# Attention and butterfly feed-forward layer on one core: the output projection moved from step 11 to behind the products with V of step 9, the early projection from step 10 to step 11

## What is computed

```
q, k, v = x·w_q, x·w_k, x·w_v            # 16 heads of 64
p   = softmax(q·k^T / 8 + causal mask)
att = einsum(p·v, w_o)                   # back to 128 features
x   = layernorm(x + att)
h   = butterfly_up(x·W_exp + b_exp)      # 512 features, 9 stages of 2x2 mixes
y   = butterfly_down(gelu(h + up_bias))·W_con + b_con + down_bias
out = layernorm(x + y)
```

## Time and profile before

| | |
|---|---|
| median of 3 runs | 1035.61 us |
| profiled execution, its own time | 1034.01 us |
| its span on the core | 1032.3 us |
| TensorE matmuls busy | 98% of the span |
| TensorE weight loads busy | 68% |
| VectorE, GpSimd, ScalarE busy | 75%, 73%, 59% |
| mean granted TensorE clock | 0.998 |

### The profile page before, as it was taken

How to read it: one execution, slowest core, us unless ns; L and a number is a source line. 1 busy time by engine, 2 the same in 40 slices (tenths; PEclk the granted TensorE clock), 3 DMA queues, 4 the chain that set the end, 5 groups by cost and what they waited for, 6 DMA issues and landing times.

```text
span 1032.3 us, 17783 instructions
## 1 busy us (share of the span) xinstructions
PE 1007.2 (98%) x5832; PEld 698.5 (68%) x5832; DVE 777.4 (75%) x2117; ACT 613.7 (59%) x1246; POOL 750.5 (73%) x715
## 2 busy tenths in 40 slices
PE   7899999999999999999999999999999999999997
PEld 5566676676766676676666766667666766765697
DVE  7867777777777777877788787877778788775456
ACT  4555665566655656666556656666656556665544
POOL 5767888777778887777778887777778887777510
PEclk9999999999999999999999999999999999999999
DMA  5332222233222222232222222332222222320002
GB/s 154 99 99 67 53 69 57 52 83 84 63 63 62 65 70 55 63 83 64 74 72 62 61 54 54 83 83 63 64 62 71 65 56 60 84 63 22 22 11 72
DMA packets 48602, 68.71 MB, mean 67 GB/s; under 512 B 15191, under 2 KB 25083, under 8 KB 48510
## 3 DMA queue, kind: packets, MB, share of 16 engines
q1 hardware_dynamic: 48510, 67.57, 25.4%
HBM read 31.11 MB, written 2.36 MB: 32 GB/s over the span
## 4 chain that ended last, share of the span: by engine, by line
PE 92%; DVE 3%; DMA 2%; ACT 1%; issue 1%; SPq 0%; POOL 0%; POOLq 0%; ACTq 0%
PE O L754 25%; PE WORK L666 14%; PE SC L727 13%; PE SC L733 13%; PE WORK L679 6%; PE WORK L714 3%; PE WORK L639 3%; PE WORK L638 3%; PE WORK L637 3%; PE WORK L815 2%; PE WORK L647 1%; PE WORK L648 1%; PE WORK L649 1%; DVE WORK L1034 1%; DMA R<-RROW 1%
## 5 line engine op out<-in xcount | busy, mean ns | idle before, releaser
L906 ACT ACTIVATE PR<-SC 128x512 f32<-128x512 f32 (+3 forms) x768 | 352.6, 490 | 267.9 <-PE SC L733 242.0
L549 POOL TENSOR_TENSOR SUM<-SUM,PR 128x1024 f32<-128x1024 f32 (+3 forms) x256 | 419.3, 1638 | 14.9 <-ACT PR L906 1.0
L1034 DVE CUSTOM_DVE_ANT_0 WORK<-WORK,CMASK 128x128 f32<-128x128 f32 (+3 forms) x512 | 239.5, 514 | 64.7 <-PE WORK L666 64.6
L727 PE MATMUL SC<-QH,KHL 128*128 128x512 f32 (+3 forms) x768 | 269.2, 356 | 4.2 <-ACT PR L906 4.0
L733 PE MATMUL SC<-QL,KH 128*128 128x512 f32 (+3 forms) x768 | 261.6, 346 | 2.8 <-DMA QL<-NROW 2.8
L534 POOL TENSOR_SCALAR_AFFINE_SELECT PR<-PR 128x256 f32<-128x256 f32 x256 | 105.7, 414 | 192.3 <-ACT PR L906 192.2
L666 PE MATMUL WORK<-KHL,QH 128*128 128x512 f32 (+3 forms) x768 | 224.8, 359 | 2.3 <-DMA KH<-KHL 1.6
L754 PE MATMUL O<-PR,VLO 128*64 128x512 f32 (+3 forms) x1024 | 199.9, 522 | 1.8 <-DVE OT L1121 1.8
L727 PEld LDWEIGHTS SC<-QH,KHL 128*128 128x128 f32 x768 | 145.2, 189 | 62.7 <-ACT PR L906 30.5
L666 PEld LDWEIGHTS WORK<-KHL,QH 128*128 128x128 f32 x768 | 135.4, 189 | 54.0 <-issue 32.6
L1037 DVE TENSOR_REDUCE MP<-WORK 128x1 f32<-128x512 f32 x256 | 164.3, 684 | 4.9
(11 more groups left out here) (134 smaller groups left out, 1103.7 us busy)
## 6 DMA issues: line engine op xcount, KB each, us to landing
QH<-QH SPq DMA_DIRECT2D x128, 128.0 KB, 2.3
KH<-KHL SPq DMA_DIRECT2D x128, 128.0 KB, 2.3
R<-RROW SPq DMA_DIRECT2D x64, 256.0 KB, 3.9
SW<-in_L_ffn_up_weights_dram SPq DMA_DIRECT2D x9, 512.0 KB, 4.4
SW<-_L_ffn_down_weights_dram SPq DMA_DIRECT2D x9, 512.0 KB, 4.4
out_dram<-X SPq DMA_DIRECT2D x7, 256.0 KB, 2.3
X<-in_L_attn_x_BSE_dram SPq DMA_DIRECT2D x3, 512.0 KB, 4.4
X<-in_L_attn_x_BSE_dram SPq DMA_DIRECT2D x2, 256.0 KB, 2.9
```

What stands on the lines that cost most here:

```text
L549: nc.gpsimd.tensor_tensor(total, total, prob(unit, s), ALU.add).then_inc(add_done, 1)
L727: nc.tensor.matmul(dst, KHL[:, par, h, kt * P:(kt + 1) * P], QH[:, par, h, q0:q0 + n], start=True, stop=False)
L906: nc.scalar.activation(prob(unit, s)[:, h, :], SC[use % NSC][:, 0:n], ACT.Exp, scale=K ** -0.5).then_inc(exp_done, 1)
L1034: op = nc.vector.tensor_tensor_reduce(cols, cols, CMASK[:, CH - n:], 1.0, LOWEST, ALU.add, ALU.max, cell)
```

## The change

Two entries of the hand-written order move. In units 0 to 29 the early projection stands behind the scores of step 11, and no longer behind those of step 10. The output projection stands late in step 9, that is directly behind the products with V of steps 4 to 6, and no longer behind the scores of step 11. No instruction is added or taken away. All engines walk through the same table, so ACT's two copies of the early projection and DVE's readout of both move with them, and both take another of the four WORK banks.

```
-FILL[10] = [[], [("proj", 0, 0)], []]
+FILL[11] = [[], [("proj", 0, 0)], []]
 COMPOSE_AFTER = [4, 5, 9]
 RECIP_AFTER = 2
 SCALE_AFTER = 6
-OUT_AT = ((11, 1), (11, 2))
+OUT_AT = ((9, 2), (9, 2))
```

## The result

The median is 1071.68 us (1071.09 to 1072.06, 4 runs) against 1035.61 us before (1035.30 to 1036.40, 4 runs): a ratio of 1.0353, 95% interval 1.034 to 1.0365. The forecast was 1070.3 us. The profiled execution took 1071.44 us, its span 1069.7 us, 37.4 more than before.

What follows compares the result with a forecast made beforehand. TensorE, busy 98% and issuing all the time, bounds the kernel, so waits add in full: 28 units at 1.18 us (33.0) + 1.7 (unit 30) + 0 = 34.7, on 1035.6 gives 1070.3 us; range 1050 to 1079.

Steps and rivals of the forecast that it cites:

- R4: Rival: hidden room in TensorE's matmul distances swallows the waits, no difference, 1036 us; chance 0.04.
- (a): Middle units: uncovered step 11 waits for step 10's exponential, starting 0.97 us after it; costs 0.56 us a unit.
- (b): Early projection's ACT copies precede step 0's exponentials, so step 1 waits; 0.68 us a unit, 0.44 ahead of step 1.
- R1: Rival: only step 11 waits, the copies fit ACT's pause; 0.48 us a unit, 1051 us; chance 0.12.
- (c): Output projection's new place removes one change of format on TensorE; gain of 0.08 us a unit.
- R3: Rival: TensorE's change of format decides and neither wait shows; faster, 1033 us; chance 0.05.
- No growth further down: Behind the second projection the delay doesn't grow, given 3.1 us slack at the norm; 0, other end 0.4 us a unit.
- R2: Rival: POOL or DVE's readout falls behind by 0.4 us a unit, + 11 us, 1081 us; chance 0.09.
- Unit 30: Output projection no longer ahead of unit 31, whose norm waits for POOL's later additions; +1.7 us, between 0 and 1.8.
- Units 0 and 1: An existing wait behind the copies goes while new waits come, of one size; 0, between -1.5 and +1.2 us.
- The page against the row: Skill page's ACT figures give 1.13 us for two copies, row 1.19; page's sum 1.7 us lower; rows decide.
- Idle time before L727: TensorE's idle time before the scores' first matmuls grows from 4.2 us to some 14 us, put down to ACT.

Runs made afterwards that it cites:

- e4: Full change, but two of the early projection's three matmuls stand behind step 10 and the third behind step 11; 1059.13 us, ratio 1.0235.
- e3: Full change, but ACT makes its two copies of the early projection behind step 0's exponentials, TensorE's order unchanged; 1052.91 us, ratio 1.0177.
- e6: Full change with output projection of units 30 and 31 as before, early projection behind step 10, a later k projection behind step 11; 1037.18 us, ratio 1.0018.
- e7: As e6, but the output projection stays behind step 11 as in the kernel before; 1035.96 us, ratio 1.0004.
- e2: Kernel before with only the early projection moved, behind step 11; output projection stays behind step 11; 1049.45 us, ratio 1.0141.

## Why the prediction was right, point by point

- *TensorE bounds, and waits add up in full.* Right. The time grew by what the stretch and unit 30 show: 35.0 + 2.0 + 0.4 us. R4 (hidden room) falls: both waits of a unit cost their whole length, with weight loads busy for only 65% of the span.
- *(a) step 11's wait.* Put at 0.97 us and 0.56 for its scores; measured 0.95 and 0.55 (546.54 to 547.09). e4 takes it away with a cover, all but 0.10 us.
- *(b) the copies ahead of step 0's exponentials.* Put at an exponential at 3.63, step 1 at 4.28 and the end at 5.22; measured 3.67, 4.32, 5.26. e3 takes it away by ACT's order alone. R1 (only step 11 waits) is what e3's kernel would be, and falls for this one.
- *(c) the gain of 0.08 us.* Wrong: net it is about 0. The shorter slot is there at step 0 (0.23 for 0.31), but the output projection takes 1.81 us behind the products with V, not the 1.76 that I carried over (543.78 to 545.59), and the early projection's first matmul, now behind 128-column scores, has a slot of 0.28 us, not 0.23. This last slot also speaks against the cause that I gave. It has no change of format ahead of it, only narrow matmuls, and still is 0.05 us longer. So up to 0.05 of the 0.08 us may be the price of narrow matmuls ahead; then it didn't fall away but went to the narrow matmuls' new neighbour. No run separates the two. Both costs together are 0.10 us a unit; 0.05 of it lies in the stretch and makes 5.22 into 5.26, the other 0.05 in the output projection. Over all units the forecast's 1.18 is short by 0.07, 2.0 us in 28 units. This is most of the 2.7 us between 34.7 and 37.4. R3, which built on this gain, falls with it.
- *No growth further down.* Right. The extra time of a unit from norm to norm (1.25) is that of the stretch and the output projection (1.22 + 0.05). R2 falls.
- *Unit 30.* Put at 1.7, measured 2.0 us. Unit 31's norm waits 1.88 us for POOL, where it waited 0.39 before:

```profile
975.77 0.45 PE L727 MATMUL SC<-QH,KHL 128*128 128x384 f32 x1
...
978.27 1.07 PE L714 MATMUL WORK<-SUM,ONES 128*32 128x512 f32 x8 [1.88 <-POOL SUM L549]
```

  e6, which leaves the output projection of units 30 and 31 in place, has 24.8 us there as before.
- *Units 0 and 1.* Put at 0, measured +0.4.
- *The median.* It came out only 1.4 us above the forecast, though the sum was 2.7 us short. The difference is luck: the profiled execution before lay 1.6 us under its median, which the forecast added, and the one after lies only 0.2 us under.
- *The page against the row.* ACT's two copies took 1.20 us (rows above), 1.19 before, not the 1.13 us that I had worked out as an estimate from the Trainium skill (ScalarE: Activation LUTs, What ACT_TABLE_LOAD costs). The measurement decides.
- *Idle time before L727.* Put at 14 us in all, measured 19.0. The forecast's own figures give more than it said: 28 x (0.24 + 0.23) = 13.2 us come on top of the 4.2. Most of the remaining 1.6 us fits the wait ahead of step 1, which shows 0.31 us beyond the drain and not 0.23.

## What to carry to other kernels

In a hand-written order, a piece of work is also the cover of the dependency around it: before it moves, name what it hides at its old place, and read the price of that place bare, in a unit that happens to lack the piece. Look at the evacuations that move with it too, since an in-order engine may then make them ahead of the instruction that the bottleneck waits for; half of this loss was in ACT's order, and two edits whose costs are 42 and 14 us alone gave 36 together. Measure waits on a pipelined engine from start to start, because its idle column showed less than half of them here.

## What the runs showed of the hardware that was not expected

The slot that a matmul takes depends on what stands ahead of it. The same 16 records of the output projection take 1.70 us behind 512-column float32r matmuls (e7; e2 too), 1.76 behind 128-column ones (528.01 to 529.77), and 1.80 to 1.81 behind true-float32 products with V (e6, after), each time within 0.01 us in all middle units. The whole difference is in the first of the 16: its slot is 0.11, 0.16 or 0.21 us in the single records of the traces, and the other fifteen are alike. A 512-column projection takes 0.28 us for its first matmul behind 128-column scores (547.09 to 547.37) and 0.24 for the next. What in the weight loads or in the formats makes this wasn't tried.
